# Last mixture of experts: GpSimd waits at every fourth indirect DMA of the second scatter and of the first return gather

## The reference, cut to what matters

```python
def _L3_ffn_ref(x, Wg, bg, W1, b1, W2, b2):
    gate_scores = x @ Wg + bg
    _, idx = jax.lax.top_k(gate_scores, K)
    mask = jax.nn.one_hot(idx, E, dtype=x.dtype).sum(axis=-2)
    xf = x.reshape(-1, Dv)
    mf = mask.reshape(-1, E)
    h = jax.nn.gelu(jnp.einsum('td,edh->teh', xf, W1) + b1[None], approximate=False)
    y = jnp.einsum('teh,ehd->ted', h, W2) + b2[None]
    out = jnp.einsum('ted,te->td', y, mf)
    return out.reshape(Bv, Sv, Dv)

x = x + _L3_ffn_ref(_layernorm(x, axis=-1), ...)
```

## Time and profile before

| what | value |
|---|---|
| median of three timed runs | 3129.7 us (3127.84 to 3139.87) |
| span of the profiled execution | 3331.1 us |
| start of `sorted_moe`'s first instructions in it | about 3062 us |
| TensorE busy over the span | 2524.9 us, 76% |
| VectorE / ScalarE / GpSimd busy | 2094.1 / 1309.8 / 721.2 us |

### The profile page before, as it was taken

How to read it: one execution, slowest core, us unless ns; L and a number is a source line. 1 busy time by engine, 2 the same in 40 slices (tenths; PEclk the granted TensorE clock), 3 DMA queues, 4 the chain that set the end, 5 groups by cost and what they waited for, 6 DMA issues and landing times. The chain is left out here.

```text
span 3331.1 us, 50319 instructions
## 1 busy us (share of the span) xinstructions
PE 2524.9 (76%) x18840; PEld 1620.7 (49%) x18840; DVE 2094.1 (63%) x4114; ACT 1309.8 (39%) x2407; POOL 721.2 (22%) x756
## 2 busy tenths in 40 slices
PE   6477999999999999965566178587649989971542
PEld 5334555555555555545255167344326666641542
DVE  6737787778788878856646397654743547761212
ACT  4333444444444444424555004232224444451431
POOL 0000000000000000010064630166610033306244
PEclk7688999999999999987689557698879978885766
DMA  4431112222221121113223101000012221111333
GB/s 76 130 107 42 49 49 49 55 60 53 50 49 49 49 49 49 46 40 121 67 77 75 43 17 18 13 5 5 5 32 70 52 50 41 41 33 56 94 87 93
DMA packets 189058, 178.78 MB, mean 54 GB/s; under 512 B 83700, under 2 KB 162177, under 8 KB 185977
## 3 DMA queue, kind: packets, MB, share of 16 engines
q1 hardware_dynamic: 168064, 137.00, 16.5%
q0 software_dynamic: 20768, 38.75, 4.8%
HBM read 139.11 MB, written 43.64 MB: 55 GB/s over the span
## 5 line engine op out<-in xcount | busy, mean ns | idle before, releaser
L3557 PE MATMUL hy_ps<-hy_uT,hy_win 128*128 128x512 f32 x1152 | 499.3, 594 | 0.0
L3557 PEld LDWEIGHTS hy_ps<-hy_uT,hy_win 128*128 128x128 f32 x1152 | 217.9, 190 | 283.0 <-issue 272.2
L2469 POOL DMA_DIRECT2D ek_w<-ek_src x32 | 17.8, 556 | 1162.6 <-DVE ek_dst L2491 1162.6
L3619 PE MATMUL hy_ps<-hy_wo,hy_yg 128*128 128x512 f32 x512 | 239.6, 613 | 14.5 <-ACT XNP L3762 8.7
L3055 PE MATMUL er_c<-XNG 128*128 128x400 f32 x480 | 184.0, 540 | 0.0
L3619 PEld LDWEIGHTS hy_ps<-hy_wo,hy_yg 128*128 128x128 f32 x512 | 94.2, 193 | 125.6 <-issue 99.3
L2690 PE MATMUL f_px<-XNG 128*128 128x40 bf16 x736 | 69.0, 266 | 98.2 <-DVE XNG L2605 66.0
L3841 DVE TENSOR_TENSOR_SCAN XNG<-XNG,hy_fx 128x2048 f32<-128x2048 f32 x32 | 141.6, 4425 | 3.0 <-issue 0.4
L2988 POOL DMA_INDIRECT er_gone<-er_nodes,er_sidx x120 | 123.7, 1031 | 36.6 <-issue 36.3
L3055 PEld LDWEIGHTS er_c<-XNG 128*128 128x128 f32 x480 | 97.6, 209 | 69.5 <-issue 14.5
L946 DVE TENSOR_TENSOR f_hg<-f_hs,f_gb 128x640 f32<-128x640 f32 x64 | 52.7, 825 | 109.9 <-ACT f_hs L928 91.3
(11 more groups left out here) (698 smaller groups left out, 6123.4 us busy)
## 6 DMA issues: line engine op xcount, KB each, us to landing
XNG<-hy_decays SPq DMA_DIRECT2D x32, 1024.0 KB
hy_rb<-hy_inverse SPq DMA_DIRECT2D x128, 128.0 KB, 3.5
f_gb<-gate_rows SPq DMA_DIRECT2D x16, 640.0 KB, 5.1
g_KB<-g_keys SPq DMA_DIRECT2D x32, 320.0 KB
f_xg<-f_rows SPq DMA_DIRECT2D x54, 128.0 KB
f_ys<-f_ysl SPq DMA_DIRECT2D x54, 128.0 KB
f_y<-f_ysl SPq DMA_DIRECT2D x47, 128.0 KB
f_rows<-in_x_dram POOLq DMA_DIRECT2D x2, 2560.0 KB, 16.0
```

What stands on the lines that cost most here:

```text
L3557: mm = pe.matmul(p[:], win[:, t, m * 128:(m + 1) * 128], uT[:, t, :], start=(t == 0), stop=(t == KT - 1))
L3619: mm = pe.matmul(PS[4 + q % 2][:], yg[:, t, q * 128:(q + 1) * 128], wo[:, t, :], start=(t == 0), stop=(t == KT - 1))
```

## The change

`sort` gets an argument `burst`. With it, GpSimd waits before every fourth indirect DMA of the scatter until all that it has sent of this half have landed; `sorted_moe` passes 4, `sorted_router` passes nothing, so the first scatter is as before. In the return gather the parts of the second half (`last`) keep the old wait. In parts 0 to 3 GpSimd waits at the groups t = 0, 2 and 4 until all gathers sent so far have landed (at t = 0 of part 0 nothing has been sent). Each group is two DMAs, so a part goes out as 4, 4 and 2.

```diff
-    def sort(self, pool, h):
+    def sort(self, pool, h, burst=None):
         for t in range(h * self.TH, (h + 1) * self.TH):
+            sent = 2 * (t - h * self.TH)
+            if burst is not None and sent > 0 and sent % burst == 0:
+                pool.wait_ge(self.sorted[h], 16 * sent)
             for c in range(2):
...
+    BURST = 4
...
             for h in range(1, ex.HALVES):
-                ex.sort(pool, h)
+                ex.sort(pool, h, BURST)
...
+                last = n >= PARTS - PARTS // ex.HALVES
                 for t in range(CT):
-                    if n > 0 and t == CT // 2:
+                    if last and n > 0 and t == CT // 2:
                         pool.wait_ge(c_in[(n - 1) % NC_], 32 * CT * ((n - 1) // NC_ + 1))
+                    if not last and t % (BURST // 2) == 0:
+                        if t > 0:
+                            pool.wait_ge(c_in[n % NC_], 32 * (CT * (n // NC_) + t))
+                        elif n > 0:
+                            pool.wait_ge(c_in[(n - 1) % NC_], 32 * CT * ((n - 1) // NC_ + 1))
```

## The result

The changed kernel takes 3157.3 us (median of 8 runs, 3145.8 to 3171.0), the kernel before 3128.8 us (median of 8 runs beside them, 3115.4 to 3144.0). The ratio is 1.0089, with a 95% interval of 1.0062 to 1.0116: 28.6 us slower (19 to 36 us). The forecast was 3075 us in a range of 3056 to 3142, so the sign was wrong and the time lies 15 us outside the range.

A forecast was written before the change was run, and what follows sets the result against it. The prediction held that matmul news is delayed while GpSimd sends without pause; pauses costing +9 and +12 us would let tiles through, starting the last gathers at 3216.4 instead of 3271.04: 3129.7 - 54.6 = 3075 us, range 3056 to 3142.

The forecast's parts named there:

- What bounds the kernel now: Last mixture: no engine bounds it while GpSimd sends; news of ended matmuls does not arrive during sends without a pause.
- Something holds the chain up: Scatter and first return gather: matmul news arrives only 3.9 and 5.8 us after GpSimd's last send is over.
- rival B: Last stage: the holding belongs to the profiled execution, so the change only costs, +9 us, 3139 us; chance 0.26.
- It is the nearest row: Second scatter: two tiles pass per burst of four, taken from the first mixture, with quiet of 1.3 us against 1.24.
- the sum: Whole change: last gathers start at 3216.4 instead of 3271.04, -54.6 us, timed median 3075 us.
- The pauses themselves: GpSimd's new waits: 9 in the scatter at 1.0 us, +9 us; 11 in the gather at about 1.1 us, +12 us.
- Tile 27's rows are wanted only when tile 21 is done, so the later landing is covered: Second scatter: tile 21 is done after 3123.4, when the scatter lands, so its later landing costs nothing.
- up to 6 us if that cover went: Second scatter: cost of its later landing if work on the first 27 tiles did not cover it, up to 6 us.
- if the quiet is longer than 1.5 us, the pauses are dearer: Sign in the changed kernel's profile: quiet above 1.5 us, where 1.3 was forecast, means pauses cost more than priced.
- if the last gathers start right behind the first ones, GpSimd has become the bound: Sign in the changed kernel's profile, at the last gathers: no gap after the first gathers means GpSimd sets the end.
- A: Scatter and gather: pauses release nothing, all stays held, and both delays are on the path, +21 us, 3151; chance 0.12.
- 0.62: Whole kernel: the chance given to a result faster by more than half a percent, 0.53 + 0.04 + 0.05.

The follow-up runs named there:

- the second profile: The kernel before, unchanged, profiled and timed again: 3126.2 us against 3129.0 (ratio 0.9984), profiled span 3123.6 us.
- e6_last_gather: The kernel before with the waits put into the second return gather (last 40 gathers) alone: 3149.4 us against 3124.7 (ratio 1.0065).

## Why the prediction was wrong, step by step

**What bounds the kernel now: wrong for the timed runs.** "Something holds the chain up" was read correctly from the earlier trace rows, but from an execution that the timed runs do not resemble. The one sign of it was in the first line of the page against the table of times, 3331.1 against 3129.7 us. I had seen it, had worked out in rival B that 92 of the 201 us would come from this stage (the second profile has 94 us less there), and still gave it 0.26. The argument against it, that nothing says recording holds up TensorE alone, was no evidence: the number of 201 us had to have a place, and I offered no other.

**"It is the nearest row": this step carried the sign, and it failed.** Two tiles for each burst came from the earlier trace rows, rows of the same disturbed execution. The quiet of 1.24 us there was the holding itself seen from GpSimd, not a pause that cured it. Undisturbed, that stage has 0.30 us between sends and no pairs. There was nothing to release, so nothing of the gain in the sum was to be had. What the change does in an execution of the held kind was not measured, since none came again; for that state the forecast is neither confirmed nor refuted.

**The pauses themselves: right in kind, too small.** Priced at 1.0 and 1.1 us for each wait, +9 and +12. Measured, less the 0.30 us of a free send: 1.94 - 0.30 = 1.64 us nine times, +15; 2.22 - 0.30 = 1.92 eleven times, +21. I took a landing 2.2 us after the send's start as the moment of the next start. In fact the next start is on average 0.96 + 1.94 = 2.9 us after the last send's start in the scatter, and 3.2 us in the gather.

Two rows were misread for it. The 2.2 us of the earlier trace rows are of the 40 sends of the first scatter, which have nothing beside them; the view has no landing for the second. The 2.27 us of the earlier trace rows are of the last gathers, when the tiles are done, and not of the first return gather. The semaphore updates in the changed kernel's trace take the rest apart. The last update before each wait's end comes 2.2 to 3.6 us after the start of the last send in the scatter (mean 2.64), and 2.5 to 4.1 us in the gather (mean 2.94); the next send starts 0.27 us after it every time (0.26 in the gather). So two terms were missing: these 0.27 us, and landings that come later while tiles are fetched and stored. Where nothing runs beside it, a wait of the scatter costs 1.53 - 0.30 = 1.2 us, as the last two of the changed kernel show (the tiles' last transfer is issued at 2998.74); one beside the tiles costs up to 2.6:

```profile
2990.33 0.95 POOL L1393 DMA_INDIRECT f_rows<-XNG,f_pidx  x1 [2.94 <-DMA f_rows<-XNG,f_pidx]
...
3009.24 0.96 POOL L1393 DMA_INDIRECT f_rows<-XNG,f_pidx  x1 [1.53 <-DMA f_rows<-XNG,f_pidx]
```

The Trainium skill ("DMA: Bandwidth & Descriptors", table of the two cost components) gives about 2.0 us fixed plus the bytes over 436 GB/s, an estimate of 2.15 us for 64 KB. The trace agrees for the first scatter's transfers, which have nothing beside them (median 2.2 us), and less so for the gathers without tiles beside them (median 2.5 us in e6_last_gather); the waits beside the tiles had landings of up to 3.6 us in the scatter and 4.1 in the gather.

**"Tile 27's rows are wanted only when tile 21 is done, so the later landing is covered": wrong.** This step looked at tile 27's own rows and not at what stands behind them in two queues. Tile 27 enters TensorE's queue two tiles ahead of its turn, so results 25 and 26 wait for the landing; and on SP the stores of tiles 22 to 26 stand behind its fetch. With them waits the start of the return gather. The cover was not there to begin with: in the kernel before, SP issues that fetch at the landing, 51.6 us after the scatter's start, and about 0.9 us were to spare. So nearly all of the 15 us of pauses went through to the start of the gather (61.9 to 77.2). The sentence gave "up to 6 us if that cover went"; taking the coupling out gave back 11 to 13 us. The code said it: `turned(i+2)` ahead of `hidden(i+1)` and `outer(i)` on TensorE, and `fetch(i+6)` ahead of the store of tile i+1 on SP.

**The chain at the end.** Before, GpSimd's last send of the first gather and result 53 fall together (110.7 and 110.8), and the last gathers start 3.6 us after that send. Now GpSimd is last, with result 53 done 22 us earlier. So the 21.1 us of waits and about 1 us of longer sends, less the 2.4 us of slack that was there, move the last gathers by 72.3 - 52.4 = 19.9 us after the gather's start. With the 15.3 us at its start that is 35.2 us for the last gathers; the stage has +34.3. The forecast's signs "if the quiet is longer than 1.5 us, the pauses are dearer" and "if the last gathers start right behind the first ones, GpSimd has become the bound" both came true.

**The rivals.** B had the right premise: nothing is held, the change only costs. Its size was wrong, +9 instead of 29 to 35 us, because it let the scatter's 9 us vanish (it started the gather at 3126.0, moved by nothing) and used the low price. With the coupling and the measured price it comes to +35, but these are numbers read after the result. A arrived at a closer time, 3151 us, since in it both terms were on the path; but its reason, news that stays held, was not there. The rule named beside it (the Trainium skill, "SBUF — State Buffer", section "SBUF: two separate sides", no slowing between DMA and compute) fits the undisturbed profiles: in all eleven the tiles come every 1.975 us beside the scatter's sends, and in the second profile TensorE is busy for 10.00 of 10 us at a DMA share of 0.64. The chances were thus laid on the wrong question: 0.62 rested on a single profile being typical.

## What to carry to other kernels

Compare the profiled span with the timed runs before reading anything else. If they differ by more than the runs do among themselves, find the stages that hold the difference, and take no mechanism and no price from them; a second profile is worth more than a fine reading of the first. A wait for everything that has been sent empties the pipe: price it as the time from the start of the last send to the next start (here 2.5 us in the scatter with nothing beside it, 2.9 to 3.2 us beside the tiles, and not the 2.2 us of a landing), and take a landing from the stretch that is to be changed. If a limit is wanted, wait for what was sent a burst earlier, which cost nothing in the scatter here. Where work of one half is interleaved with the next (a transpose two tiles ahead, a fetch ahead of stores), follow the order on every engine that handles the next half's data to see what stands behind it.

## What was not expected of the hardware

One execution of the twelve profiled ones held back the news of ended matmuls (12 and 14 us in the pairs of the earlier trace rows), all in the three stages in which GpSimd sends indirect DMAs beside TensorE's work; its span was 207.5 us longer than another of the same kernel, and no timed run was near it. What brings an execution into that state stays open. It could not be brought about at will, so nothing was tried on it.

Undisturbed, 40 indirect DMAs of 64 KB, sent one per 1.26 us, and tiles at 1.975 us each ran beside each other without any loss to the tiles: result 24 was at 54.8 to 57.4 us after the scatter's start in all eleven later profiles, with no pause, with one after eight, four or two sends, and with a window of eight. What was lengthened is the DMA's own landing, from 2.2 us to as much as 3.6 us beside the tiles' fetches and stores.
